# Feature walk of a four-layer graph network: over its first 200 steps GpSimd makes the fourth column indicator, VectorE one of four row distances, ScalarE three

## The reference, cut to what matters

```python
edge_index = jnp.stack([src, dst])            # 103125 edges, dst sorted
h = relu(layernorm(x)); x = x + L0(h, edge_index, ...)
h = relu(layernorm(x)); x = x + L1(h, edge_attr_8, edge_attr_64, edge_weight, ...)
h = relu(layernorm(x)); x = x + L2(h, ..., src, dst)
h = relu(layernorm(x)); x = x + L3(h, ..., src, dst)
# L0, L2, L3: e = leaky_relu(s1[src] + s2[dst]); softmax over a node's edges; weighted sum of rows
```

## Time and profile before

| what | value |
|---|---|
| time, median of 3 runs | 4114.31 us (4111.0 to 4128.04) |
| profiled execution, its own time | 4111.32 us |
| its span in the profile | 4109.5 us |
| VectorE busy | 3713.2 us, 90% of the span |
| TensorE busy | 3061.0 us, 74% |
| GpSimd busy | 1854.6 us, 45% |
| ScalarE busy | 1778.3 us, 43% |
| first 200 steps of the walk | 42.6 to 420.3 us |

### The profile page before, as it was taken

The page is one execution under the profiler, slowest core; times in us unless marked ns, Lnnn a source line. Parts: engine busy times, 40 slices in busy tenths (PEclk is TensorE's granted clock), DMA queues, the critical chain, the costliest instruction groups (busy, mean ns, idle before and its releaser), DMA issues. The chain is left out here.

```text
span 4109.5 us, 129459 instructions
## 1 busy us (share of the span) xinstructions
PE 3061.0 (74%) x53233; PEld 1908.0 (46%) x53233; DVE 3713.2 (90%) x5525; ACT 1778.3 (43%) x3392; POOL 1854.6 (45%) x3678
## 2 busy tenths in 40 slices
PE   5666566466469999999892799999999993186166
PEld 2111111222146666666661577777777773123122
DVE  8999999799888988898889899999999995897898
ACT  5999988477423333333331222222222220274085
POOL 0100455200177777777771577777777774000000
PEclk9889977678789999999996899999999996598599
DMA  4763799866345555555551233333333332464554
GB/s 166 300 269 154 277 359 355 297 210 209 102 131 152 156 156 158 152 159 155 155 153 42 77 107 106 109 107 108 104 104 109 105 105 91 169 234 156 195 190 177
DMA packets 412794, 680.07 MB, mean 165 GB/s; under 512 B 75245, under 2 KB 353069, under 8 KB 400561
## 3 DMA queue, kind: packets, MB, share of 16 engines
q1 hardware_dynamic: 336736, 559.22, 41.1%
q0 software_dynamic: 39568, 78.78, 7.0%
q10 hardware_dynamic: 35904, 33.79, 2.8%
HBM read 399.92 MB, written 271.65 MB: 163 GB/s over the span
## 5 line engine op out<-in xcount | busy, mean ns | idle before, releaser
L730 POOL DMA_INDIRECT arena<-h_table,srci x808 | 775.3, 960 | 246.4 <-issue 233.3
L824 PE MATMUL banks<-arena 128*128 128x500 bf16 x1440 | 434.2, 436 | 273.8 <-DVE arena L1491 212.3
L1780 DVE TENSOR_TENSOR arena<-banks,arena 128x1024 f32<-128x1024 f32 x404 | 492.4, 1219 | 40.8 <-PE banks L931 35.8
L1902 DVE TENSOR_TENSOR arena<-banks,arena 128x1024 f32<-128x1024 f32 x404 | 494.6, 1224 | 37.4 <-PE banks L1049 0.7
L1894 DVE TENSOR_TENSOR arena<-banks,arena 128x1024 f32<-128x1024 f32 x404 | 490.7, 1214 | 6.8 <-ACT arena L1339 5.6
L1180 ACT ACTIVATE arena<-arena,h 128x128 bf16<-128x128 f16 x1440 | 454.4, 386 | 83.7 <-DVE arena L1504 43.1
L1049 PE MATMUL banks<-arena 64*64 64x256 f32 x6464 | 446.1, 388 | 0.9 <-DVE arena L1902 0.9
L1068 PE MATMUL banks<-arena 64*64 64x128 f32 x12928 | 429.6, 269 | 8.8 <-issue 8.2
L942 PE MATMUL banks<-arena 64*64 64x128 f32 x12928 | 427.1, 270 | 0.0
L1479 DVE TENSOR_SCALAR arena<-arena,agg 128x500 bf16<-128x500 f16 x1440 | 410.9, 350 | 0.2
L824 PEld LDWEIGHTS banks<-arena 128*128 128x128 bf16 x1440 | 127.5, 105 | 579.5 <-DVE arena L1479 439.8
(11 more groups left out here) (296 smaller groups left out, 5619.8 us busy)
## 6 DMA issues: line engine op xcount, KB each, us to landing
arena<-c_flat SPq DMA_DIRECT2D x75, 1562.5 KB, 6.7
slots<-arena SPq DMA_DIRECT2D x90, 1000.0 KB, 4.7
arena<-hs_dump SPq DMA_DIRECT2D x404, 128.0 KB
arena<-mask_rows SPq DMA_DIRECT2D x50, 781.2 KB, 4.3
arena<-in_edge_attr SPq DMA_DIRECT2D x202, 128.0 KB
arena<-placed SPq DMA_DIRECT2D x202, 128.0 KB
xs_dump<-arena SPq DMA_DIRECT2D x202, 128.0 KB
hs_dump<-arena SPq DMA_DIRECT2D x202, 128.0 KB
```

Of the source, the lines that this page charges most:

```text
L730: pool.indirect_dma_start(out=xs[t % NX][:, k * D:(k + 1) * D], out_offset=None, in_=h_table, in_offset=bass.IndirectOffsetOnAxis(ap=srci[ ...
L824: last = pe.matmul(ps[4 + r % 2][:, 0:BW], row_hot[r][:, k * P:(k + 1) * P], col_hot[r][:, k * BW:(k + 1) * BW], start=k == 0, stop=k == K ...
L1780: V.tensor_tensor(bt[h].rearrange("p (s n) -> p s n", s=4), banks[:, 4 * COLS:6 * COLS].rearrange("p (s n) -> p s n", s=4), h2k[t % 3].rea ...
L1902: V.tensor_tensor(vt[h], banks[:, 2 * COLS:4 * COLS], dt_[h], ALU.mult).then_inc(vt_sb, 1)
```

## The change

For the first `SHARED` = 200 of 360 steps, three pieces of a step change hands:

- the fourth column indicator (k = 3, 500 columns) goes from VectorE to GpSimd, as the same `tensor_scalar`, announced by a new semaphore `side_hot` that TensorE waits for;
- the first row indicator (k = 0, 128 columns) goes from ScalarE to VectorE, as one `tensor_scalar` with two operations, add and is_equal to 0, straight into `row_hot`;
- ScalarE makes three distances, and its Relu covers 384 columns in place of 512.

GpSimd's 25 row fetches are now issued between its indicators, fetch b after the indicator of step 34 + 4b. Steps 200 to 359 are as before. (The diff also drops `fence` and tests of `isinstance(..., int)`; all loops were written out already, so that these lines did nothing.)

```diff
+SHARED = 200
+FIND = 34
...
-            pool.wait_ge(rows_ready, 1)
-            find_rows(0, NB)
+            pool.wait_ge(left_go, 1)
+            for s in range(SHARED):
+                at(counted_ps, s - 3, pool)
+                pool.tensor_scalar(col_hot[s % 4][:, (KE - 1) * BW:KE * BW], iota16[:, 0:BW], col_key[:, KE - 1, bass.ds(s, 1)], None,
+                                   ALU.is_equal).then_inc(side_hot, 1)
+                if s >= FIND and (s - FIND) % 4 == 0 and (s - FIND) // 4 < NB:
+                    if s == FIND:
+                        pool.wait_ge(rows_ready, 1)
+                    find_rows((s - FIND) // 4, (s - FIND) // 4 + 1)
             pool.wait_ge(row_counted, NB)
...
                 pe.wait_ge(hot_ready, s + 1)
                 pe.wait_ge(left_ready, s + 1)
+                if s < SHARED:
+                    pe.wait_ge(side_hot, s + 1)
                 at(summed, s - 1, pe)
...
                 at(left_ready, s - 3, act)
-                for k in range(KE):
+                for k in range(1 if s < SHARED else 0, KE):
                     last = act.activation(apart[r % 4][:, k * P:(k + 1) * P], iota16[:, 0:P], ACT.Abs, bias=minus_key[:, k, bass.ds(s, 1)])
...
-                act.activation(row_hot[r], apart[r], ACT.Relu, bias=ones[:, 0:1], scale=-1.0).then_inc(left_ready, 1)
+                cols = slice(P if s < SHARED else 0, KE * P)
+                act.activation(row_hot[r][:, cols], apart[r][:, cols], ACT.Relu, bias=ones[:, 0:1], scale=-1.0).then_inc(left_ready, 1)
...
                 at(counted_ps, s - 3, dve)
-                for k in range(KE):
+                if s < SHARED:
+                    V.tensor_scalar(row_hot[r][:, 0:P], iota16[:, 0:P], minus_key[:, 0, bass.ds(s, 1)], 0.0, ALU.add, ALU.is_equal)
+                for k in range(KE - 1 if s < SHARED else KE):
                     made = V.tensor_scalar(col_hot[r][:, k * BW:(k + 1) * BW], iota16[:, 0:BW], col_key[:, k, bass.ds(s, 1)], None, ALU.is_equal)
```

More of the change, by code:

```diff
@@ L310, in build @@
         phase = sem("phase")
-        pe_go, pool_go, dve_go = sem("pe_go"), sem("pool_go"), sem("dve_go")
         dve_steps = sem("dve_steps")
@@ L315, in build @@
         walk_in, key_ps, key_sb = sem("walk_in"), sem("key_ps"), sem("key_sb")
-        hot_ready = sem("hot_ready")
+        hot_ready, side_hot = sem("hot_ready"), sem("side_hot")
         counted_ps, summed = sem("counted_ps"), sem("summed")
@@ L336, in build @@
         row_maxed, bias_ready, scored = sem("row_maxed"), sem("bias_ready"), sem("scored")
-        sp_go = sem("sp_go")
         masked, maxed = sem("masked"), sem("maxed")
@@ L380, in at @@
         def at(sem_, value, eng):
-            if not (isinstance(value, int) and value <= 0):
+            if not (value <= 0):
                 eng.wait_ge(sem_, value)
-        def fence(eng, go):
-            eng.sem_inc(go, 1)
         def panel(g):
@@ L450, in flush @@
                 sp.wait_ge(summed, q * 4 + 4)
-                if not isinstance(q, int):
-                    fence(sp, sp_go)
                 sp.dma_start(slots_v[q], fbuf[par]).then_inc(flushed[par], 16)
@@ L494, in one @@
                 def one(b, r, quarter=None, half=None):
-                    if not (isinstance(b, int) and b < n):
+                    if b >= n:
                         sp.wait_ge(used, b + (base + 1 - n))
-                        if not isinstance(b, int):
-                            fence(sp, sp_go)
                     sp.dma_start(tiles[r % n], rows[bass.ds(b, 1), :, :].rearrange("o p f -> (o p) f")).then_inc(arrived[r % n], 16)
@@ L819, in step @@
                 pe.wait_ge(left_ready, s + 1)
+                if s < SHARED:
+                    pe.wait_ge(side_hot, s + 1)
                 at(summed, s - 1, pe)
-                if not isinstance(s, int):
-                    fence(pe, pe_go)
                 for k in range(KE):
@@ L1225, in l0_mask @@
                 act.wait_ge(c4_in[r], quarter * 16 + 16)
-                if not (isinstance(b, int) and b < 2):
+                if b >= 2:
                     act.wait_ge(row_maxed, b - 1)
@@ L1487, in total @@
                 at(summed, s, dve)
-                if isinstance(s, int) and s == 0:
+                if s == 0:
                     add = V.tensor_copy(out=fbuf[0][:, 0, :], in_=ps[4][:, 0:BW])
@@ L1628, in l0_top @@
                 dve.wait_ge(masked, b + 1)
-                if not isinstance(b, int):
-                    fence(dve, dve_go)
                 m = mx[r]
@@ L1760, in fill @@
                 if c == 0:
-                    before, keep = (seed[:, :], None) if isinstance(t, int) and t == 0 else (xd[1 - par][:, (K - 1) * D:K * D], 0)
+                    before, keep = (seed[:, :], None) if t == 0 else (xd[1 - par][:, (K - 1) * D:K * D], 0)
                     if keep is None:
```

## The result

The changed kernel takes 4188.09 us (median of 4 runs, 4182.48 to 4194.73) against 4113.43 us (median of 4) of the kernel before: a ratio of 1.0181, 95% interval 1.0166 to 1.0196. It is slower by 75 us. Its profiled execution took 4194.73 us by its own time, with a span of 4192.8.

The account below looks back on a forecast made before the run. VectorE at 1.68 us a step was taken to bound the walk, ScalarE close behind. Exclusion's +17 or 18 us minus 4 for ScalarE made +13: 4124 profiled, 4127 median, range 4088 to 4166.

Parts of the forecast that it names:

- What bounds the kernel: First 200 steps: VectorE full at 1.68 us a step, ScalarE nearly full at 1.78; gains or losses pass to the end.
- Undisturbed gain of 23 us: First 200 steps, engines not disturbing each other: VectorE's step 1.59 us saves 19 us, ScalarE's relief 4; chance 0.20.
- Exclusion: First 200 steps: VectorE's indicator group and GpSimd's indicator shut each other out for their whole length, costing 17 or 18 us.
- T = 0.65 us: Assumed time of GpSimd's 500-column indicator in each of the first 200 steps; gives a VectorE step of 1.77 us.
- 1.02 as the upper end: Longest time allowed for GpSimd's indicator, from a two-input operation at 500 columns; step 1.96 us, +52 us in all.
- the recorded estimate beside the rival: The skill's measured GpSimd loop, 769 ns for 512 elements; by it the loss would be near 25 us.
- slow compare: Rival: GpSimd's indicator takes 0.73 us or more, losing over 20 us; centre 4145 to 4150, chance 0.33.
- GpSimd becomes the limit: Rival: TensorE's waits for GpSimd's indicator set the step, over 2.4 us; +150 us, about 4265, chance 0.05.
- d = (T - 0.28) / 2: Delay d per step of VectorE's indicator group when GpSimd's indicator takes T; 0.185 us at 0.65.
- GpSimd's indicator over 0.75: Sign in the changed profile that the forecast is wrong: GpSimd's indicator was expected to take 0.6 to 0.7 us.
- a stretched instruction while GpSimd runs: Sign that the forecast is right: a VectorE instruction starting while GpSimd runs is stretched or late by 0.1 to 0.3 us.
- the hole of a whole GpSimd instruction inside a group: Sign of a wrong forecast: VectorE's group interrupted for GpSimd's whole instruction; step 2.2 us and more, over +100 us.

Follow-up runs that it names:

- the one-port pair: Changed kernel with row indicator back on ScalarE and VectorE's three column indicators reading five gapped blocks: 1.0059 without GpSimd's indicator, 1.0065 with it, against the kernel before.
- The copy: Changed kernel with GpSimd's compare replaced by a copy of the same 500 columns, float16 in, bfloat16 out: ratio 1.0032 to the kernel before.

## Why the prediction was wrong, point by point

**What bounds the kernel: right.** VectorE at 1.68 us a step, and what was lost by step 200 (70.7 us) passed through to the end (83 us between the profiled executions, 75 by the medians).

**Undisturbed gain of 23 us: right in kind, a little high.** 17 us (12 to 22) by the run with the indicator left out; VectorE's step was 1.59 as worked out, and the row indicator 0.17.

**Exclusion: right in kind, wrong in extent.** It was put as likely, from the DMA issues that ended 0.13 us behind a group, and the one-port pair shows it. But the sum let GpSimd hold VectorE through its whole instruction, and the trace shows a hold at its two ends with a gap in between.

**The step that failed is the price of GpSimd's indicator: T = 0.65 us, with 1.02 as the upper end.** It measured 1.52 us undisturbed; the recorded estimate beside the rival, from a loop of 769 ns, was half of that as well. The upper end was no bound: I drew it from a two-input operation, on the argument that one input can't cost more than two, and took the engine's reads for what it spends its time on. The copy shows that the reads cost 0.60; the two-operand arithmetic of this form costs 0.92 more. The rival "slow compare" had the right mechanism, chance 0.33, but ended at 1.02 us and 4166 as well, so that the range missed by 22 us. The condition for the rival "GpSimd becomes the limit", T beyond 1.5, was met, and its price of +150 us was not: TensorE waited for GpSimd once.

**The formula d = (T - 0.28) / 2 failed too, the other way.** For T = 1.52 it gives d = 0.62 and, over 200 steps, 200 x (0.62 - 0.09) - 4 = +102 us. Measured were d = 1.96 - 1.59 = 0.38 in plain steps, 0.45 in the mean of all 200 (90 us), and +75. The formula lets GpSimd hold VectorE until its instruction ends. In the trace of the steps at 1.97 the hold ends 0.5 us after GpSimd's start, VectorE's group runs through, and GpSimd, held 0.45 us in turn (1.97 against 1.52), finishes beside the total. With the right T it would have forecast slower by 2.5%. That its step of 1.96 for T = 1.02 is the measured step is luck: T was too small and the hold too long.

**What would show it:** of the signs that I named, "GpSimd's indicator over 0.75" and a stretched instruction while GpSimd runs came true; the hole of a whole GpSimd instruction inside a group did not.

## What to carry to other kernels

Before work goes to an idle GpSimd, measure that very form of instruction there: a `tensor_scalar` with a per-partition number cost 1.52 us for 500 columns where VectorE needs 0.26 and a GpSimd copy 0.61, and no other form bounds it. Then look at what VectorE runs beside it: here the indicators in dense form were stretched (and some counts with two inputs, 1177 ns in the mean for 1047), the totals that read PSUM were not. What VectorE is relieved of must exceed what is held (here 0.26 relieved less 0.17 taken over, against 0.38 held). If an engine at 100% busy completes fewer instructions, as here 94 for 116, compare mean durations and not waits; and before taking one step's timeline for all of them, count how many steps look like it.

## What the runs showed of the hardware

- GpSimd and VectorE did not exclude each other for a whole instruction, as the rule of the Trainium skill ("SBUF — State Buffer", "Who interferes with whom") has it. A 1.52 us instruction held VectorE 0.38 us a step in plain steps and let a group of about 0.94 us through in its middle; the measurement decides here. It held VectorE at its two ends (all 19 indicators that started 0.05 to 0.25 us into one, all 26 at 0.85 to 1.05, one of 39 between). What GpSimd does there was not tried.
- A memset of 500 columns, which reads nothing, costs a plain step nothing that shows (1.59 us): it runs beside the total, and the row indicator that meets its last part takes 0.28 us in place of 0.24. Its 8 us (0.9978 against 0.9959) lie in the other steps: 34 to 134 take 188.8 us against 181.9. GpSimd and VectorE in that run:

```profile
391.10 0.52 POOL L691 MEMSET arena<- 128x500 bf16 x1 [1.06 <-PE banks L818]
...
391.38 0.28 DVE L1472 TENSOR_SCALAR arena<-arena,h 128x128 bf16<-128x128 f16 x1
```

- The same 500 columns cost VectorE 0.26 us from a dense source and 0.38 from five blocks with gaps between them.
